# Loading the third projection weight in the attention stage, and sharing x's pair buffers with the stage that follows

## The chip, the cores and the metric

The program runs on one core of one Trainium2 chip. The metric is device time in microseconds (us) of one execution, as the median of a few runs. Five engines work side by side and meet only through semaphores: TensorE (PE, with its weight loads listed apart as PEld), VectorE (DVE), ScalarE (ACT), GpSimd (POOL) and SyncE (SP), which here issues most of the DMAs. POOL issues the DMAs that gather rows by an index.

## The reference, cut to what matters

x has 8192 rows of 512 numbers. The output is x plus two branches of xn, the layer norm of x.

```python
def step(carry, qkv):            # branch 1: 64 rows at a time, 16 heads
    M, z = carry
    q, k, v = qkv                # xn @ W_q.T, xn @ W_k.T, xn @ W_v.T
    ...
    return ((M_new, z_new), A_s)
...
weights = (x @ router_w)[..., 0] + router_b[0]   # branch 2: a router picks rows
topv, topi = jax.lax.top_k(weights, k)           # k = 1024 of 8192
...
x_sel = x[bidx, sel_idx]
hn = rmsnorm(x_sel, ln1)
q = rope(heads(hn @ wq), pos_sel)
kk = rope(heads(hn @ wk), pos_sel)
v = heads(hn @ wv)
... softmax attention among the selected rows, then
x1 = x_sel + o
x2 = x1 + jax.nn.gelu(rmsnorm(x1, ln2) @ w1) @ w2
```

The change concerns `wq`, `wk` and `wv` of branch 2, which have 512 x 512 numbers each.

## The kernel before, in words

The kernel is a row of stages, with a barrier of all engines between one and the next. `infini_attention` is the first and longest. It takes x in 32 pairs of tiles (two tiles of 128 rows), counts and chooses the rows of branch 2 on the way, and ends with `idx`, the chosen row numbers. `feed_forward` follows, and its first stage is called the projection stage here. It has eight tiles t = 0 to 7 of 128 chosen rows. For each it normalises the rows (`moments`, `scaled`), turns them round on PE (`turn_h`), splits them into a high and a low part (`high_h` on ACT, `low_h` on DVE), multiplies by the three weights (`project` on PE, 12 matmuls for each weight), and turns key and query by their angles (`turned` on DVE). The key then goes in high and low parts through `stacks` on PE. Beside that, POOL gathers rows of the causal mask, PE turns them (`masks`), ACT copies them out, and SP writes them to `mask_columns`. After it come softmax attention and the MLP.

Every weight of the projection stage exists as a high part (a rounding to float32r, made by ACT) and a low part (the raw weight less the high part, made by DVE), since PE multiplies high by high, low by high and high by low. So DVE and ACT have one pass each over 128 x 2048 numbers for each weight.

Before the change, the key and query weights are loaded by `next_weight` near the end of the attention stage, into `xin` and `xn`, x's pair buffers, which are free by then. ACT makes both high parts there (`next_high`), and DVE makes the key's low part. The stage's buffers then vanish. The projection stage therefore loads the raw query weight again and the raw value weight for the first time:

```python
for n, d in enumerate((wq_d, wv_d)):
    sp.dma_start(raw[n], d.rearrange("(c p) n -> p c n", p=P)).then_inc(s_wd[n], 16)
```

`raw[0]` lies in `xs2` (eight stage rows of 512 numbers, which later hold the turned query rows and then the MLP's raw weights), and `raw[1]` in `x1T`, whose first half is also `mcol`, the place of the mask columns. So SP's first write of mask columns waits for both low parts (`s_low`).

The order on an engine is the order in which the code is written. On DVE the projection stage opens with

```python
moments(0, 1)
scaled(0)
moments(1, 2)
low_h(0)
query_low()
angles(0)
value_low()
roots(0)
turns(0)
```

and then runs the loop over the tiles, which begins with `turned(t, KEY)`. Inside t = 0, after `low_h(1)`, stand `moments(2, 4)`, `roots(1)` and `angles(1)`. `moments(t)` waits for the gathered rows of tile t, and `angles(0)` and `angles(1)` wait for the gathered positions of tiles 0 and 1, and 2 to 7. POOL issues, one after the other: rows 0, rows 1, positions 0, positions 1, rows 2 to 7, positions 2 to 7, and then the mask rows, the first two without a wait and each later one when PE has turned the one two before it.

Of the kernel before, what the change touches and what calls it, by code (L numbers as in the profile page):

```python
# [7 lines left out]
F32 = mybir.dt.float32  # L8
# [16 lines left out]
P = 128  # L25
# [14 lines left out]
def infini_attention(nc, x, wqT, wkT, wvT, woT, beta, router_w, router_b, wq_d, wk_d, out, ident, inv, thr, idx,  # L40
                     held):
# [6 lines left out]
    T, D = x.shape  # L48
# [25 lines left out]
    with ExitStack() as ctx:  # L74
# [23 lines left out]
        xin = sb("xin", [P, 2, TILES, D])  # L98
        xn = sb("xn", [P, 2, TILES, D])
# [74 lines left out]
        next_raw = [t[:, :, :, :].rearrange("p a b n -> p (a b) n") for t in (xin, xn)]  # L174
# [16 lines left out]
        s_cw = [sem(f"s_cw{n}") for n in range(2)]  # L191
# [109 lines left out]
        def _(sp):  # L301
# [25 lines left out]
            def half(m, p, first=False, ln=True, stage1=True):  # L327
# [11 lines left out]
                if stage1:  # L339
                    shift_v(m, 1 - p)  # L340
                if AHEAD + m + 1 < NB:
                    sp.wait_ge(s_e, m + 1)
                    sp.dma_start(xe[:, :, :], x_t[AHEAD + m + 1]).then_inc(s_xe, 16)
# [13 lines left out]
            sp.wait_ge(s_od, 32 * NB)  # L357

# [927 lines left out]
def feed_forward(nc, x, maskT, positions, router_w, router_b, wq_d, wv_d, wo_d, w1_d, w2_d, ln1, ln2, ident, inv, thr, idx,  # L1286
                 held,
                 out, cols_dram):
# [20 lines left out]
    with ExitStack() as ctx:  # L1309
# [14 lines left out]
        xs2 = sb("xs2", [P, Q, D])  # L1324
# [18 lines left out]
        with ExitStack() as c1:  # L1343

            raw = (xs2[:, 0:G, :], x1T[:, 0:2, :].rearrange("p g (a n) -> p (g a) n", n=D))
# [46 lines left out]
            s_wd = [sem("s_wdq", c1), sem("s_wdv", c1)]  # L1392
# [31 lines left out]
            def _(sp):  # L1424
                sp.dma_start(l1[:, :], ln1.broadcast_to([P, D])).then_inc(s_l1, 16)
                for n, d in enumerate((wq_d, wv_d)):
                    sp.dma_start(raw[n], d.rearrange("(c p) n -> p c n", p=P)).then_inc(s_wd[n], 16)
                sp.dma_start(rw[:, :], router_w.rearrange("d a -> a d").broadcast_to([P, D])).then_inc(s_rw, 16)
                sp.dma_start(rb[:, :], router_b.broadcast_to([P, 1])).then_inc(s_rw, 16)
                for u in range(UNITS):  # L1430
                    if u == 0:
                        sp.wait_ge(s_low, 2)
# [44 lines left out]
            def _(act):  # L1477
# [48 lines left out]
                def value_high():  # L1526
                    act.wait_ge(s_wd[1], 16)
                    act.activation(vhigh[:, :, :], raw[1], ACT.Copy).then_inc(s_high, 1)

                act.activation(cos[:, 0, 0:1], ident[:, 0:1], ACT.Sin)  # L1530
                high_h(0)
                value_high()
# [26 lines left out]
            def _(dve):  # L1559
# [73 lines left out]
                def query_low():  # L1633
                    dve.wait_ge(s_wd[0], 16)
# [28 lines left out]
                dve.tensor_scalar(c2[:, 1, :], cidx[:, :], 2.0, 1.0, ALU.mult, ALU.add).then_inc(s_ci, 1)  # L1663
                moments(0, 1)
# [3 lines left out]
                query_low()  # L1668
                angles(0)
                value_low()  # L1670
# [761 lines left out]
def build(nc, x, wqT, wkT, wvT, woT, beta, maskT, positions, router_w, router_b, wq, wk, wv, wo, w1, w2, ln1, ln2,  # L2432
# [4 lines left out]
    with ExitStack() as ctx:  # L2437
# [6 lines left out]
        infini_attention(nc, x, wqT, wkT, wvT, woT, beta, router_w, router_b, wq, wk, out, ident, inv, thr, idx,  # L2444
# [45 lines left out]
```

## Time and profile before

| what | value |
|---|---|
| median of 3 runs | 1964.27 us (1963.94 to 1964.94) |
| the profiled execution, its own time | 1966.73 us |
| its span from first to last instruction | 1965.0 us |
| mean granted TensorE clock | 0.981 of full speed |
| PE busy | 1861.8 us (95%) |
| DVE busy | 1443.1 us (73%) |
| ACT busy | 875.6 us (45%) |
| POOL busy | 151.0 us (8%) |

Times in the rows below are us from the first instruction. The attention stage ends at about 1288, and the projection stage runs from there to about 1418. A timeline row gives the start, the length, the engine, the line, the operation, what it writes and reads, how many instructions were merged, and in brackets how long the engine sat idle before it and what released it. An "issue" in brackets is idle time in which the engine waited for nothing that the profile shows.

### The profile page before, as it was taken

How to read it: one execution, taken by the hardware profiler on the slowest of the kernel's cores; microseconds unless marked ns; L12 is line 12 of the kernel's file. 1: busy time of each engine (PE TensorE's matmuls, PEld its weight loads, DVE VectorE, ACT ScalarE, POOL GpSimd, SP SyncE). 2: the span in 40 equal slices, each digit the busy share in tenths (PEclk: the TensorE clock that was granted, in tenths of full speed). 3: DMA queues.
4: the chain of work that ended last, by engine and by line, in shares of the span. 5: the costliest groups of instructions: out<-in, count | busy, mean ns of one | idle time of the engine just before them, and what ended most of it. 6: DMA issues, size and time to landing. Idle time of an engine off the chain costs nothing. (4 is left out here: it accounts for less than half of the span.)

```text
span 1965.0 us, 72355 instructions
## 1 busy us (share of the span) xinstructions
PE 1861.8 (95%) x32380; PEld 1579.7 (80%) x32380; DVE 1443.1 (73%) x3478; ACT 875.6 (45%) x1494; POOL 151.0 (8%) x179
## 2 busy tenths in 40 slices
PE   6999999999999999999999999859899999888998
PEld 6888888888888888888888888647777777667997
DVE  6888788888887777787777777557588788876222
ACT  4343444334443434444344344225588788754110
POOL 1000000000000000000000000141100000001000
PEclk9999999999999999999999999779999999999999
DMA  4112111211121121112111211036500000015000
GB/s 146 46 46 70 59 52 46 78 57 46 57 73 41 36 57 41 41 35 57 46 36 35 62 41 62 30 129 192 157 32 13 12 12 23 12 44 161 11 12 22
DMA packets 65668, 109.52 MB, mean 56 GB/s; under 512 B 4736, under 2 KB 25232, under 8 KB 65360
## 3 DMA queue, kind: packets, MB, share of 16 engines
q1 hardware_dynamic: 59584, 85.74, 14.0%
q0 software_dynamic: 5776, 19.15, 3.1%
q8 instruction: 257, 4.21, 0.9%
q14 instruction: 51, 0.42, 0.1%
HBM read 60.31 MB, written 27.26 MB: 45 GB/s over the span
## 5 line engine op out<-in xcount | busy, mean ns | idle before, releaser
L1021 PE MATMUL proj<-xnT_high,held 128*128 128x256 f32 x1536 | 235.2, 289 | 2.8 <-DVE xnT_low L749 2.1
L1021 PEld LDWEIGHTS proj<-xnT_high,held 128*128 128x128 f32 x1536 | 203.7, 191 | 8.8 <-DVE xnT_low L749 2.6
L425 POOL TENSOR_TENSOR As<-T 128x512 f32<-128x512 f32 x64 | 84.1, 1315 | 1178.9 <-DVE T L844 1178.9
L1021 PE MATMUL proj<-xnT_low,held 128*128 128x256 f32 x1024 | 163.7, 281 | 0.0
L2017 DVE CUSTOM_DVE_ANT_0 Sm<-Sp,held 128x1023 f32<-128x1023 f32 x128 | 155.5, 1215 | 8.4 <-DVE xs L2005 2.0
L1915 ACT ACTIVATE Sm<-Sm,least 128x1023 f32<-128x1023 f32 x128 | 146.7, 1146 | 14.2 <-DVE least L2017 13.4
L1021 PEld LDWEIGHTS proj<-xnT_low,held 128*128 128x128 f32 x1024 | 140.2, 190 | 0.0
L2070 PE MATMUL Sp<-KS,held 128*128 128x512 f32 x256 | 94.4, 451 | 29.8 <-DVE least L2017 25.6
L484 ACT ACTIVATE Pq<-Pq 128x1024 f32<-128x1024 f32 x64 | 67.9, 1061 | 121.2 <-DVE Pq L813 120.9
L464 ACT ACTIVATE QT<-proj 128x512 f32<-128x512 f32 x64 | 38.1, 595 | 181.7 <-PE proj L1021 181.7
L1967 DVE COPY PTs<-Tp 128x512 f32<-128x512 f32 x128 | 88.3, 690 | 29.6 <-PE Tp L2082 29.1
L443 ACT ACTIVATE DV<-proj 128x512 f32<-128x512 f32 x64 | 38.2, 597 | 159.9 <-PE proj L1031 159.9
L2291 PEld LDWEIGHTS Sp<-held,KS 128*128 128x128 f32 x768 | 96.7, 193 | 9.2 <-issue 3.6
L2291 PE MATMUL Sp<-held,KS 128*128 128x256 f32 x768 | 98.4, 285 | 5.4 <-DVE held L2276 2.7
L1888 ACT ACTIVATE PTs<-Tp 128x512 f32<-128x512 f32 x128 | 76.1, 595 | 52.7 <-PE Tp L2078 49.5
L2351 PE MATMUL yb<-w2m,held 128*128 128x512 f32 x384 | 94.5, 396 | 0.0
L464 ACT ACTIVATE KT<-proj 128x512 f32<-128x512 f32 x64 | 38.3, 598 | 104.6 <-PE proj L1021 104.6
L2351 PEld LDWEIGHTS yb<-w2m,held 128*128 128x128 f32 x384 | 70.3, 189 | 14.8
L2078 PE MATMUL Tp<-ident,Sm 128*128 128x128 f32 x512 | 81.0, 281 | 1.0 <-ACT PTs L1888 0.9
L1021 PE MATMUL proj<-xnT_high,wk_low 128*128 128x256 f32 x512 | 81.3, 280 | 0.4 <-issue 0.4
L813 DVE TENSOR_TENSOR Pq<-S,mx 128x1024 f32<-128x1024 f32 x64 | 78.4, 1225 | 2.2
L1184 PE MATMUL proj<-wo_high,AT_high 128*128 128x512 f32 x256 | 77.8, 426 | 1.7 <-DVE AT_low L756 1.6
(322 smaller groups left out, 4360.1 us busy)
## 6 DMA issues: line engine op xcount, KB each, us to landing
VS<-DV SPq DMA_DIRECT2D x64, 264.0 KB, 3.9
xin<-in_x SPq DMA_DIRECT2D x32, 512.0 KB, 4.8
out_rows<-xu SPq DMA_DIRECT2D x64, 256.0 KB, 2.0
mask_columns<-x1T SPq DMA_DIRECT2D x16, 512.0 KB
xs<-in_w SPq DMA_DIRECT2D x16, 512.0 KB, 4.0
xe<-in_x SPq DMA_DIRECT2D x15, 512.0 KB, 3.5
QT<-in_wqT SPq DMA_DIRECT2D x1, 1024.0 KB, 6.1
KT<-in_wkT SPq DMA_DIRECT2D x1, 1024.0 KB, 9.3
```

Source lines behind the costliest of these rows:

```text
L425: pool.tensor_tensor(As[:, :], T1[:, :], T2[:, :], ALU.add).then_inc(s_as, 1)
L464: act.activation(raw[:, pn, 2 * k:2 * k + 2, :], v, ACT.Copy, scale=scale)
L813: dve.tensor_tensor(Pq[:, :, :, :].rearrange("p g j k -> p j g k"), s_half(a), mx[:, :, :].rearrange("p j (g o) -> p j g o", o=1).broadcas ...
L1021: ins = pe.matmul(bank[:, g * BT:g * BT + BT], w[hw][:, c, o:o + P], xnT[hx][:, c, :], start=n + c == 0, stop=n == 2 and c == G - 1)
L1184: ins = pe.matmul(bank[:, :], AT[ha][:, g, :], wo[hw][:, g, :], start=n + g == 0, stop=n == 2 and g == G - 1)
L1915: act.activation(Sm[:, h % 4, 0:KC], Sm[:, h % 4, 0:KC], ACT.Exp, bias=least[:, h % 4:h % 4 + 1], scale=-1.0, accum_out=rsum[:, b, h:h + 1 ...
L1967: dve.tensor_copy(PTs[:, slot(t, h), 4:8, :], Tp[1][:, :].rearrange("p (k q) -> p k q", k=4))\
L2017: dve.tensor_tensor_reduce(Sm[:, h % 4, 0:KC], Sp[h % 2][:, 0:KC], mc[:, b, 0:KC], 1.0, 3.0e38, ALU.add, ALU.min, least[:, h % 4:h % 4 + 1])\
L2070: ins = pe.matmul(Sp[h % 2][:, u * 512:u * 512 + 512], QS[:, h, :], KS[:, h, u * 512:u * 512 + 512], start=True, stop=True)
L2078: ins = pe.transpose(Tp[0][:, k * P:k * P + P], Sm[:, h % 4, k * P:k * P + P], ident[:, :])
L2291: ins = pe.matmul(self.hb[n % 4][:, e * self.NT:e * self.NT + self.NT], self.w1[hw][:, c, f * P:f * P + P], self.xT[hx][:, c, :], start=m ...
L2351: ins = pe.matmul(yb[(u % 2) * QU + q][:, :], gT[hg][:, n % 4, e, q * P:q * P + P], w2[hw][:, f, :], start=f + m == 0, stop=f == FC - 1 an ...
```

## The change

`xs2` is now made ahead of both functions and handed to both. In the attention stage its first four rows are `xin` and its last four are `xn`. The raw query weight, loaded into `xn`, therefore survives the end of the attention stage. A third load brings the raw value weight into the place of `xin`, once ACT has made the key's high part and DVE its low part. The projection stage issues no weight loads, ACT makes the value's high part before `high_h(0)`, and DVE makes both low parts before everything else that is long. SP's first write of mask columns no longer waits for the low parts.

```diff
-        xin = sb("xin", [P, 2, TILES, D])
-        xn = sb("xn", [P, 2, TILES, D])
+        xin, xn = [xs2[:, 2 * TILES * i:2 * TILES * i + 2 * TILES, :].rearrange("p (b a) d -> p b a d", a=TILES)
+                   for i in range(2)]
...
-        next_raw = [t[:, :, :, :].rearrange("p a b n -> p (a b) n") for t in (xin, xn)]
+        next_raw = [xs2[:, 0:G, :], xs2[:, G:2 * G, :], xs2[:, 0:G, :]]
...
+                if m == NB - 1:
+                    sp.wait_ge(s_ch, 1)
+                    sp.wait_ge(s_cl, 1)
+                    next_weight(VALUE, wv_d)
                 if AHEAD + m + 1 < NB:
...
             sp.wait_ge(s_od, 32 * NB)
+            sp.wait_ge(s_cw[VALUE], 16)
...
-            raw = (xs2[:, 0:G, :], x1T[:, 0:2, :].rearrange("p g (a n) -> p (g a) n", n=D))
+            raw = (xs2[:, G:2 * G, :], xs2[:, 0:G, :])
...
-                for n, d in enumerate((wq_d, wv_d)):
-                    sp.dma_start(raw[n], d.rearrange("(c p) n -> p c n", p=P)).then_inc(s_wd[n], 16)
...
-                    if u == 0:
-                        sp.wait_ge(s_low, 2)
...
                 def value_high():
-                    act.wait_ge(s_wd[1], 16)
                     act.activation(vhigh[:, :, :], raw[1], ACT.Copy).then_inc(s_high, 1)
...
+                value_high()
                 high_h(0)
-                value_high()
                 waves(0)
...
                 def query_low():
-                    dve.wait_ge(s_wd[0], 16)
...
+                query_low()
+                value_low()
                 moments(0, 1)
                 scaled(0)
                 moments(1, 2)
                 low_h(0)
-                query_low()
                 angles(0)
-                value_low()
                 roots(0)
                 turns(0)
```

On DVE, at the head of the projection stage, the order before was this. `wq_low` and `wv_low` are the two low parts, `cidx` and `c` the clipped indices, `hn` the normalised rows of a tile, `hnT` their turned form, `fb` the banks of PSUM, and `pos` the positions.

```order
L1661 TENSOR_SCALAR cidx<-idx 128x8
L1662 TENSOR_SCALAR c<-cidx 128x8 [waits s_st]
L1663 TENSOR_SCALAR c<-cidx 128x8 [waits s_st]
L1610 BN_STATS stats<-xs 128x6 [waits s_xg0]
L1613 BN_AGGR mv<-stats 128x2 [waits s_st]
L1630 SCALAR_TENSOR_TENSOR hn<-xs,mv,ln 128x512 [waits s_l1,s_st]
L1610 BN_STATS stats<-xs 128x6 [waits s_xg1]
L1613 BN_AGGR mv<-stats 128x2 [waits s_st]
L1643 TENSOR_TENSOR hnT<-fb,hnT 128x512 [waits s_hh,s_st]
L1635 TENSOR_TENSOR wq_low<-xs,held 128x2048 [waits s_wdq]
L1578 CAST posf<-pos 128x2 [waits s_pos0]
```

After the change the same place reads as follows.

```order
L1659 TENSOR_SCALAR c<-cidx 128x8 [waits s_st]
L1631 TENSOR_TENSOR wq_low<-xs,held 128x2048
L1635 TENSOR_TENSOR wv_low<-xs,wv_high 128x2048 [waits s_high]
L1606 BN_STATS stats<-xs 128x6 [waits s_xg0]
L1609 BN_AGGR mv<-stats 128x2 [waits s_st]
L1626 SCALAR_TENSOR_TENSOR hn<-xs,mv,ln 128x512 [waits s_l1,s_st]
L1606 BN_STATS stats<-xs 128x6 [waits s_xg1]
L1609 BN_AGGR mv<-stats 128x2 [waits s_st]
L1639 TENSOR_TENSOR hnT<-fb,hnT 128x512 [waits s_hh,s_st]
L1574 CAST posf<-pos 128x2 [waits s_pos0]
```

Both low parts moved ahead of the first wait for gathered rows (`s_xg0`), and the query's waits for no load any more.

On SP, around the barrier between the two stages, the order before was this. The rows of `out_rows` are the last stores of the attention stage.

```order
L319 DMA out_rows<-xu 128x512 [waits s_free0]
L319 DMA out_rows<-xu 128x512 [waits s_od,s_free0] x3
L74 UNCONDITIONAL_BRANCH [waits s_od]
L1423 UNCONDITIONAL_BRANCH [waits barrier_Pool_Activation_PE_DVE_SP_release]
L1425 DMA ln<-in_ln 128x512
L1427 DMA xs<-in_wq 128x4x512
L1427 DMA x1T<-in_wv 128x4x512
L1428 DMA rw<-in_router_w 128x512
L1429 DMA rb<-in_router_b 128x1
L1436 DMA mask_columns<-x1T 128x8x128 [waits s_mc,s_low]
```

After the change SP reads here as follows.

```order
L319 DMA out_rows<-xu 128x512 [waits s_od,s_free0]
L325 DMA xs<-in_wv 128x4x512 [waits s_od,s_cl,s_ch]
L319 DMA out_rows<-xu 128x512 [waits s_free0]
L319 DMA out_rows<-xu 128x512 [waits s_od,s_free0]
L74 UNCONDITIONAL_BRANCH [waits s_od,s_cw2]
L1425 UNCONDITIONAL_BRANCH [waits barrier_Pool_Activation_PE_DVE_SP_release]
L1427 DMA ln<-in_ln 128x512
L1428 DMA rw<-in_router_w 128x512
L1429 DMA rb<-in_router_b 128x1
L1434 DMA mask_columns<-x1T 128x8x128 [waits s_mc] x16
```

The value weight's load moved between the second and the third of the last four stores, and the query weight's second load is gone. The orders of PE and POOL are the same before and after.

## Rows read from the trace of the kernel before

**Rows 1.** Stretches: us; PE, PEld, DVE, ACT, POOL busy (instructions); clock, DMA share, GB/s
```profile
1290.00:1300.00 10.00, 1.12 (x4) 0.72 (x4) 2.42 (x5) 0.21 (x2) 7.56 (x9) 0.50 0.90 318
...
1311.00:1325.00 14.00, 10.17 (x46) 8.18 (x46) 12.53 (x42) 4.62 (x7) 3.14 (x4) 0.76 0.23 76
1325.00:1340.00 15.00, 14.18 (x81) 11.71 (x80) 13.81 (x42) 7.79 (x15) 2.78 (x3) 1.00 0.49 150
...
1360.00:1380.00 20.00, 19.81 (x122) 16.90 (x121) 10.95 (x22) 11.84 (x22) 4.93 (x5) 1.00 0.79 223
```

**Rows 2.** Timeline of DVE in the projection stage's first part
```profile
1289.02 0.17 DVE L1663 TENSOR_SCALAR c<-cidx 128x8 uint32<-128x8 uint32 x1
...
1296.95 0.70 DVE L1610 BATCH_NORM_STATS2 stats<-xs 128x6 f32<-128x512 f32 x1 [7.75 <-DMA xs<-in_x,idx]
...
1300.56 0.69 DVE L1643 TENSOR_TENSOR hnT<-fb,hnT 128x512 fp32r<-128x512 f32 x1 [1.09 <-issue]
1301.17 2.28 DVE L1635 TENSOR_TENSOR wq_low<-xs,held 128x2048 fp32r<-128x2048 f32 x1
1303.37 0.16 DVE L1578 CAST posf<-pos 128x2 f32<-128x2 int32 x1
...
1306.11 2.29 DVE L1639 TENSOR_TENSOR wv_low<-x1T,wv_high 128x2048 fp32r<-128x2048 f32 x1
1308.31 0.16 DVE L1619 TENSOR_SCALAR vv<-mv 128x2 f32<-128x2 f32 x1
...
1311.44 0.69 DVE L1654 TENSOR_TENSOR qa<-fb,coss 128x512 f32<-128x512 f32 x1
...
1322.34 0.17 DVE L1578 CAST posf<-pos 128x6 f32<-128x6 int32 x1
...
1333.01 0.68 DVE L1643 TENSOR_TENSOR hnT<-fb,hnT 128x512 fp32r<-128x512 f32 x1
```

**Rows 3.** Timeline of ACT there
```profile
1289.86 0.20 ACT L1530 ACTIVATE cos<-ident 128x1 f32<-128x1 f32 x1
...
1301.98 1.91 ACT L1528 ACTIVATE wv_high<-x1T 128x2048 fp32r<-128x2048 f32 x1 [1.53 <-issue]
```

**Rows 4.** Timeline of POOL there: the DMAs that it issues
```profile
1289.33 1.02 POOL L1441 DMA_INDIRECT xs<-in_x,idx  x1 [14.24 <-POOLq L74]
...
1302.29 1.98 POOL L1445 DMA_INDIRECT pos<-in_positions,cidx  x1 [0.30 <-issue]
...
1307.11 2.11 POOL L1445 DMA_INDIRECT pos<-in_positions,cidx  x1 [0.30 <-issue]
...
1312.03 0.94 POOL L1462 DMA_INDIRECT x1T<-in_maskT,c  x1 [0.30 <-issue]
```

**Rows 5.** DMA issues: what, by whom, how many, median us from issue to landing
```profile
xs<-in_x,idx POOLq DMA_INDIRECT x8, 6.2
...
held<-mask_columns,cidx POOLq DMA_INDIRECT x8, 4.4
xs<-out_rows,idx POOLq DMA_INDIRECT x8, 3.6
```

**Rows 6.** Timeline of PE there
```profile
1298.71 1.12 PE L1730 MATMUL fb<-ident,hn 128*128 128x128 f32 x4 [13.36 <-DVE hn L1630]
1301.31 6.39 PE L1747 MATMUL fb<-held,hnT 128*128 128x512 f32 x20 [1.48 <-DVE hnT L1643]
...
1314.24 0.66 PE L1730 MATMUL fb<-ident,hn 128*128 128x128 f32 x4 [2.80 <-DVE hn L1630]
1315.93 3.83 PE L1769 MATMUL fb<-ident,kst 128*128 128x128 f32 x16 [1.02 <-DVE kst L1683]
...
1323.29 1.03 PE L1722 MATMUL ft<-ident,x1T 128*128 128x128 f32 x8
```

**Rows 7.** Timeline of the attention stage's tail: one row of DVE, one of SP
```profile
1257.78 2.28 DVE L743 TENSOR_TENSOR held<-xin,held 128x2048 fp32r<-128x2048 f32 x1
...
1278.54 7.90 SPq L319 DMA_DIRECT2D out_rows<-xu  x2
```

More of the change, by code:

```diff
@@ L37, in bm, with infini_attention @@
     return t.rearrange("p (o n) -> p o n", o=1).broadcast_to([t.shape[0], m, t.shape[1]])
-def infini_attention(nc, x, wqT, wkT, wvT, woT, beta, router_w, router_b, wq_d, wk_d, out, ident, inv, thr, idx,
-                     held):
+def infini_attention(nc, x, wqT, wkT, wvT, woT, beta, router_w, router_b, wq_d, wk_d, wv_d, out, ident, inv, thr, idx,
+                     held, xs2):
     T, D = x.shape
@@ L190, in infini_attention @@
         s_wl = sem("s_wl")
-        s_cw = [sem(f"s_cw{n}") for n in range(2)]
+        s_cw = [sem(f"s_cw{n}") for n in range(3)]
         s_ch = sem("s_ch")
@@ L1283, in rotation_steps, with feed_forward @@
     return np.float32(1.0) / np.float32(10000.0) ** (np.arange(0, DK, 2, dtype=np.float32) / np.float32(DK))
-def feed_forward(nc, x, maskT, positions, router_w, router_b, wq_d, wv_d, wo_d, w1_d, w2_d, ln1, ln2, ident, inv, thr, idx,
-                 held,
-                 out, cols_dram):
+def feed_forward(nc, x, maskT, positions, router_w, router_b, wo_d, w1_d, w2_d, ln1, ln2, ident, inv, thr, idx,
+                 held, xs2, out, cols_dram):
     D = x.shape[1]
@@ L1323, in feed_forward @@
         l2 = l1
-        xs2 = sb("xs2", [P, Q, D])
         x1T = sb("x1T", [P, G, K])
@@ L1391, in feed_forward @@
             s_rw = sem("s_rw", c1)
-            s_wd = [sem("s_wdq", c1), sem("s_wdv", c1)]
             s_high = sem("s_high", c1)
@@ L2443, in build @@
                 for n in range(3)]
-        infini_attention(nc, x, wqT, wkT, wvT, woT, beta, router_w, router_b, wq, wk, out, ident, inv, thr, idx,
-                         held)
-        feed_forward(nc, x, maskT, positions, router_w, router_b, wq, wv, wo, w1, w2, ln1, ln2, ident, inv, thr, idx,
-                     held,
+        xs2 = ctx.enter_context(nc.sbuf_tensor("xs2", [P, K // P, x.shape[1]], F32))
+        infini_attention(nc, x, wqT, wkT, wvT, woT, beta, router_w, router_b, wq, wk, wv, out, ident, inv, thr, idx,
+                         held, xs2)
+        feed_forward(nc, x, maskT, positions, router_w, router_b, wo, w1, w2, ln1, ln2, ident, inv, thr, idx,
+                     held, xs2,
                      out, cols_dram)
```

## The prediction, made before the changed kernel was run

> **What bounds the kernel now.** I read first the stretches of the projection stage, then the timeline of each engine at its head. In the attention stage TensorE is busy throughout and the change takes nothing off it, so what can move lies after 1288 us. From 1290 to 1300 nothing works: PE is busy 1.12 of 10 us at half clock (0.50, 1.2 GHz), DVE 2.42, while the DMA engines are at a share of 0.90 [rows 1]. DVE sits idle 7.75 us for the first gathered rows, which land at 1296.95, and PE 13.36 us for what DVE makes of them [rows 2, 6]. Then DVE sets the pace: 12.53 of 14 us from 1311 to 1325 and 13.81 of 15 to 1340, with PE waiting for it 2.80 and 1.02 us at 1314 to 1316 [rows 1, 6]. Later PE does (19.81 of 20 us from 1360, DVE 10.95) [rows 1]. A DVE that is earlier at its first `turned` by some us should therefore hand PE an earlier start, and since all later work, masks included, follows PE, that is kept to the end. The number to find is how much earlier `turned(0, KEY)` begins, now 1311.44 [rows 2].
>
> **The change part by part.**
>
> *Attention stage, no cost.* SP waits for DVE's low part of the key, which ends at 1257.78 + 2.28 = 1260.06, and loads the value weight. Behind that wait on SP stands only the store that is issued at 1278.54, 18 us later [rows 7]. The new wait ahead of the barrier is for a load begun at 1260. The slowest landing that I have in sight is a gather's 6.2 us [rows 5]; even twice that is long past by 1288. If the 18 us of cover were gone, the store and the barrier would be late by what is missing. No instruction is added: two 1 MB loads leave the projection stage, one enters the attention stage.
>
> *DVE's two low parts move into the idle time.* They stand at 1301.17 and 1306.11, and the next starts come at 1303.37 and 1308.31, so each costs the path 2.20 us, together 4.4 us [rows 2]. In the new place, the query's low part starts when DVE ends its three index operations, 1289.02 + 0.17 = 1289.2, and ends at 1291.4. The value's needs ACT's high part: ACT is free at 1290.06 and takes 1.91 us, to 1292.0 [rows 3], so the low part runs from 1292.0 to 1294.2. DVE is then free 2.7 us before the rows landed so far.
>
> *The gathers lose their company and gain an obstacle.* POOL's first issue takes 1.02 us from 1289.33, and its rows land 6.6 us after the issue's end, at 1296.95, amid the 2 MB of weights [rows 2, 4]. The same kind of gather elsewhere, with little beside it, lands 3.6 us after its start, so some 2.65 us after its end, an issue being 0.94 us [rows 4, 5]. Against that, the two issues of position DMAs that began while DVE was inside a low part took 1.98 and 2.11 us in place of 0.94, and both ended 0.82 us after that DVE operation [rows 2, 4]. A low part now runs from 1289.2, just ahead of the first issue. I therefore let that issue end at 1291.4 + 0.8 = 1292.3 and its rows land at 1294.9. The second issue begins 0.3 us later, inside the value's low part (1292.0 to 1294.2), ends at 1295.1, and its rows land at 1297.7. Positions 0 and 1 are issued to 1296.3 and 1297.6; by the same 2.65 us (an estimate, since no row shows a position's landing) they land at 1300.2.
>
> The Trainium skill, "SBUF — State Buffer", section "SBUF: two separate sides", states the same in its rule that a DVE instruction with two SBUF inputs and a GpSimd instruction that reads SBUF lock each other out; the stretched issues agree. Its practical consequences add, marked as inferred, that a `tensor_tensor` takes only the read interface while descriptor generation needs the write interface, so that it should not stall such a DMA. By that, the first rows would not be held up; it is rival 2, and the 1.98 and 2.11 us speak against it.
>
> *The sum.* `low_h(0)` came 1300.56 - 1296.95 = 3.6 us after the first rows [rows 2], so 1298.5; `moments(1, 2)` ahead of it, about 1 us, cannot begin before 1297.7, which makes it 1298.7, ended 1299.4. `angles(0)` waits for the positions until 1300.2. It takes 1306.11 - 1303.37 = 2.74 us, and from there to `turned` it is 1311.44 - 1308.31 = 3.13 us [rows 2], so `turned(0, KEY)` begins at 1306.1 in place of 1311.4: **5.3 us earlier**. Of this, 4.4 us are the two passes and 0.9 us the earlier gathers.
>
> *Does PE follow?* It starts the first projection at 1299.4 in place of 1301.31. The whole of it ran to 1311.44 (2.80 us of idle before 1314.24) [rows 6], half clock included, so now to some 1310.0 (half clock may last longer, since it began earlier). Then `turn_h(1)` follows without its 2.80 us of waiting, and `stacks(0)` begins near 1310.7 in place of 1315.93, 5.2 us earlier. PE keeps up. The 16 transposes and the next 12 matmuls then bring it to `masks(1)` at about 1317, from 1323.29. Here a new wait comes up. POOL is 3.5 us late after its second issue, gets back the 1.04 and 1.17 us of the two stretched issues, and may lose some to DVE's shorter passes in the loop, which its issues of positions now meet; I allow 1.3 us for that, an estimate of about one stretched issue. So the first mask gather starts at about 1314.3 in place of 1312.03, and by 4.4 us it lands at 1318.5 [rows 4, 5]. PE idles 1.5 us. DVE next needs PE at `low_h(2)`, 1333.01 before and 1327.7 now [rows 2]; my PE arrives some 0.4 us ahead. The last positions land at 1316.5, and `angles(1)` needs them at 1322.34 - 5.3 = 1317.0 [rows 2]. Both covers are thin, 0.4 and 0.5 us.
>
> The sum against the profiled execution's own time is 1966.73 - 5.3 = 1961.4 us. That execution was 2.5 us above the median of the runs, so against the median it is 1964.27 - 5.3 = **1959.0 us**. A measurement of this kernel can tell about 0.2% from no change, which is 3.9 us.
>
> **The rivals.**
>
> 1. *The gathers land no earlier, only the passes are saved.* If what delays the first rows is not the weights, or both passes hold up the first issue one after the other (its end 1295.0, rows 1297.7, everything 0.8 us later), the gain is 4.4 or 3.6 us: 1959.9 to 1960.7. For it: the gap between the passes is only 0.6 us. Against it: the DMA share of 0.90 falls away with the weights [rows 1].
> 2. *The passes don't stall the issues.* The first rows land at 1290.35 + 2.65 = 1293.0, DVE takes them at 1294.2, positions are there by 1296.8, and `angles(0)` begins at 1298.6. DVE would gain 7 us, but `low_h(1)` then waits for PE, which loses time at half clock; about 6.3 us are left: 1958.0. The stretched issues speak against it [rows 4].
> 3. *PE is held at the masks and its clock falls.* After the 2.80 and 1.02 us of idle at 1311 to 1316 the granted clock of 1311 to 1325 was 0.76 on average, that is 3.4 us of 14 lost [rows 1, 6]. The forecast takes these waits away, but puts 1.5 us in their place a little later. If that brings the clock down for half as long, PE loses 1.7 us, against 0.4 us of cover; with a mask gather 0.5 to 1 us later too, the gain falls to 2.2 to 3.6 us: 1960.7 to 1962.1.
> 4. *It is hidden.* If PE were the pace from 1316 on, a DVE that is earlier would change less: PE is busy 14.18 of 15 us from 1325 [rows 1]. But PE itself is freed by the same amount, so a gain under 1 us (1963.3 and above) needs another pace, which I do not see.
> 5. *Slower: POOL's queue becomes the pace.* `angles(1)` needs the last positions, twelve issues behind positions 1. Each us that they are late beyond 1317.0 is a us on DVE. Were every one of the twelve stretched like the worst in sight (2.11 - 0.94 = 1.17 us), of which I have counted 1.3 us in all, they would be 12.7 us later, less 0.5 us of cover: 5.3 - 12.2, a loss of 6.9 us, 1971.2. It decides from 5.8 us of further delay. Against it: two of the fourteen issues after the first two were stretched that far, and the long passes are past by 1294.2.
>
> **How the numbers follow.** The forecast, gains of 4.5 to 6 us, has 0.48; rival 1 0.16; rival 2 0.08; rival 3 0.17; rival 4 0.06; rival 5 0.05 (of which a loss over 3.9 us is nearly all). Faster by over 0.2%: 0.48 + 0.08 + 0.11 of rival 1 = 0.67. The same: 0.05 of rival 1, rival 3 and rival 4 = 0.28. Slower: 0.05. The range from 1957.4 to 1962.6 reaches past rival 2 by 0.6 us and past rival 3 by 0.5 us, for other half-clock stretches that an earlier start may shift, and leaves out rivals 4 and 5 and the tails.
>
> **What would show it.** After: no weight load after the barrier; DVE in its low parts at 1289.2 and 1292.0 (counted from the same barrier); POOL's first two issues of some 3.0 and 2.5 us; first rows landed near 1295; `turned` 5.3 us earlier; a granted clock above 0.9 from 1311 to 1325; a short wait of PE for the first mask rows; and from 1360 on the same rows as before, 5.3 us earlier. The prediction is wrong if the first rows land at 1297 or later, if `angles(1)` or `low_h(2)` waits for more than 1 us, or if the attention stage itself ends at another time.

## The result, and the profile after

| | before | changed |
|---|---|---|
| median, 22 runs each on one chip | 1964.32 us (1960.91 to 1966.99) | 1968.51 us (1964.81 to 1974.94) |
| ratio, 95% interval | | 1.0020 (1.0014 to 1.0027) |
| profiled execution, span | 1965.0 us | 1965.6 us |
| mean granted TensorE clock | 0.981 | 0.979 |

The changed kernel takes 4.2 us more. The forecast was 5.3 us less, so the prediction was wrong in size and in sign here.

The barrier after the attention stage is read at DVE's first index operation. It stands at 1285.56 us here and stood at 1288.61 before. In the twenty traces of this study it lies between 1281.9 and 1288.6 (two traces of the kernel before: 1288.61 and 1285.00), so that difference is scatter. From here on, "+n" is a time in us after this barrier.

The timeline of DVE at the head of the stage, in the changed kernel, to be held against [rows 2]:

```profile
1285.56 0.17 DVE L1657 TENSOR_SCALAR cidx<-idx 128x8 uint32<-128x8 uint32 x1 [2.60 <-PEq L74]
...
1286.05 2.28 DVE L1631 TENSOR_TENSOR wq_low<-xs,held 128x2048 fp32r<-128x2048 f32 x1
1288.85 2.29 DVE L1635 TENSOR_TENSOR wv_low<-xs,wv_high 128x2048 fp32r<-128x2048 f32 x1 [0.52 <-ACT wv_high L1525]
1291.62 0.69 DVE L1607 BATCH_NORM_STATS2 stats<-xs 128x6 f32<-128x512 f32 x1 [0.48 <-DMA xs<-in_x,idx]
...
1297.06 0.17 DVE L1575 CAST posf<-pos 128x2 f32<-128x2 int32 x1 [0.98 <-DMA pos<-in_positions,cidx]
...
1305.02 0.69 DVE L1650 TENSOR_TENSOR qa<-fb,coss 128x512 f32<-128x512 f32 x1 [2.24 <-remote]
...
1312.86 0.69 DVE L1650 TENSOR_TENSOR qa<-fb,coss 128x512 f32<-128x512 f32 x1 [2.65 <-remote]
```

The head is as forecast: both low parts at once, first rows at +6.07 (before +8.34), positions at +11.5. Then `turned(0, KEY)` (1305.02) waits 2.24 us and `turned(0, QUERY)` (1312.86) 2.65 us. The releaser is given as "remote": a semaphore that the instruction waits for was updated just before it began, but no instruction that makes this update had ended within 1.5 us ahead of that. The timeline of POOL in the changed kernel, for [rows 4]:

```profile
1286.28 2.95 POOL L1439 DMA_INDIRECT xs<-in_x,idx  x1 [14.52 <-POOLq L74]
1289.53 2.46 POOL L1439 DMA_INDIRECT xs<-in_x,idx  x1 [0.30 <-issue]
...
1311.47 0.94 POOL L1460 DMA_INDIRECT x1T<-in_maskT,c  x1 [0.30 <-issue]
```

The timeline of PE there, for [rows 6]:

```profile
1303.32 1.10 PE L1743 MATMUL fb<-wq_low,hnT 128*128 128x512 f32 x4
1304.26 2.04 PE L1743 MATMUL fb<-wv_high,hnT 128*128 128x512 f32 x8
1306.13 1.10 PE L1743 MATMUL fb<-wv_low,hnT 128*128 128x512 f32 x4
1307.92 0.66 PE L1726 MATMUL fb<-ident,hn 128*128 128x128 f32 x4 [0.70 <-DVE hn L1627]
1310.27 1.09 PE L1765 MATMUL fb<-ident,kst 128*128 128x128 f32 x8 [1.68 <-issue]
1316.97 1.94 PE L1765 MATMUL fb<-ident,kst 128*128 128x128 f32 x8 [5.61 <-ACT KS L1520]
```

The timeline of ACT, where it has waited for `turn_h(1)`:

```profile
1315.17 0.60 ACT L1493 ACTIVATE hnT<-fb 128x512 fp32r<-128x512 f32 x1 [6.23 <-remote]
```

PE ends the query's last four matmuls at 1304.42, and DVE gets the bank at 1312.86. PE ends the transposes of `turn_h(1)` at 1308.58, and ACT starts on them at 1315.17, 6.6 us later, with nothing else to wait for. PE then stands still for 5.61 us, because ACT has not emptied a bank. Half clock begins 26 us after the barrier, as before the change, but lasts 10.2 us in place of 6.8 (0.63 granted from 1311 to 1325). I call this **late signals**: the work is done by its record, and those who wait for it learn of it microseconds later. POOL's last issue of its stream ends at 1312.41. The kernel before has no such row of PE here.

The trace also keeps the time of each semaphore update, and there the lateness can be read directly. The update for the query's matmuls, which end at +18.9, is recorded at +27.28, and DVE starts at +27.30. The next four updates of PE, for work that ends at +21.67 (the value), +23.02 (`turn_h(1)`), +25.36 and +25.80 (the key's transposes), are recorded at +29.52, +29.58, +29.64 and +29.70, and ACT starts at +29.61. So the four were held back and came 0.06 us apart.

### The profile page after: what moved, and what is told of

It is laid out like the page before. It is cut to its first block and busy times, and to the rows that moved or that the text cites. A ratio compares the mean times of both kernels' runs of the same rounds, so it can differ in the third digit from the quotient of the medians.

```text
span 1965.6 us, 72355 instructions
## 1 busy us (share of the span) xinstructions
PE 1864.1 (95%) x32380; PEld 1583.4 (81%) x32380; DVE 1442.9 (73%) x3478; ACT 875.7 (45%) x1494; POOL 153.6 (8%) x179
## 5 line engine op out<-in xcount | busy, mean ns | idle before, releaser
L2074 PE MATMUL Tp<-ident,Sm 128*128 128x128 f32 x512 | 82.3, 284 | 0.9 <-ACT PTs L1884 0.8
L2078 PE MATMUL Tp<-ident,Sm 128*128 128x128 f32 x512 | 79.0, 278 | 1.6 <-DVE PTs L1963 1.6
```

Source lines behind the costliest of these rows:

```text
L2074: ins = pe.transpose(Tp[0][:, k * P:k * P + P], Sm[:, h % 4, k * P:k * P + P], ident[:, :])
L2078: ins = pe.transpose(Tp[1][:, (k - 4) * P:(k - 4) * P + P], Sm[:, h % 4, k * P:k * P + P], ident[:, :])
```

## The experiments

The expectations speak of calls: a call is one session on one chip, in which some kernels and the kernel before were timed side by side, and ratios are to that. The table has what the traces showed. "Signals" counts the semaphore updates of PE, DVE and ACT that have a record at the end of their instruction (within 0.15 us), out of those that their instructions make, between +12 and +28. Of the others, some are recorded late and some not at all. The columns with the names of two operations have the time at which they begin. "Stage" runs from the barrier to the first instruction of softmax attention on DVE, and "rest" from there to the end.

| call | kernel | ratio (95%) | signals | `turned(0, KEY)` | `high_h(1)` | stage | rest |
|---|---|---|---|---|---|---|---|
| given | before | 1 | 41/50 | +22.8 | +26.3 | 132.5 | 543.9 |
| result | changed | 1.0020 (1.0014 to 1.0027) | 14/44 | +19.5 | +29.6 | 133.9 | 546.1 |
| 1 | e0 changed | 1.0022 (1.0011 to 1.0032) | 17/46 | +17.2 | +29.4 | 133.9 | 546.0 |
| 1 | e1 | 0.9999 (0.9987 to 1.0011) | 45/59 | +20.7 | +24.2 | 130.3 | 546.3 |
| 1 | e2 | 1.0021 (1.0011 to 1.0031) | 18/49 | +19.5 | +29.1 | 134.0 | 546.5 |
| 1 | e3 | 1.0001 (0.9991 to 1.0011) | 38/50 | +22.8 | +26.4 | 132.5 | 543.6 |
| 2 | e4 | 0.9989 (0.9979 to 0.9999) | 61/61 | +18.5 | +22.0 | 128.1 | 540.7 |
| 2 | e7 | 0.9977 (0.9965 to 0.9990) | 67/67 | +18.5 | +22.1 | 128.6 | 540.1 |
| 2 | e5 | 1.0015 (1.0004 to 1.0026) | 71/71 | +17.5 | +22.1 | 133.5 | 541.7 |
| 2 | e6 | 0.9969 (0.9956 to 0.9983) | 71/71 | +17.2 | +22.1 | 127.1 | 541.7 |
| 3 | e8 changed | 1.0012 (1.0003 to 1.0021) | 12/47 | +18.0 | +29.4 | 133.4 | 545.2 |
| 3 | e9 | 1.0020 (1.0011 to 1.0030) | 13/47 | +18.1 | +29.5 | 134.0 | 546.1 |
| 3 | e10 (as e6) | 0.9993 (0.9984 to 1.0002) | 18/48 | +17.3 | +26.7 | 130.9 | 545.5 |
| 3 | e11 (as e7) | 0.9992 (0.9981 to 1.0003) | 27/57 | +18.6 | +25.2 | 131.3 | 545.4 |
| 4 | e12 changed | 0.9983 (0.9970 to 0.9996) | 71/71 | +17.2 | +22.1 | 127.1 | 541.5 |
| 4 | e13 (as e5) | 1.0019 (1.0007 to 1.0031) | 73/73 | +17.0 | +22.1 | 133.5 | 541.6 |
| 4 | e14 | 0.9978 (0.9967 to 0.9990) | 73/73 | +17.0 | +22.1 | 126.9 | 541.5 |
| 4 | e15 | 0.9971 (0.9960 to 0.9983) | 71/71 | +17.2 | +22.1 | 127.1 | 541.5 |
| 5 | e16 (as e14) | 0.9987 (0.9975 to 0.9998) | 30/59 | +18.8 | +23.0 | 129.2 | 545.8 |
| 6 | e17 before | 0.9999 (0.9987 to 1.0011) | 50/50 | +22.7 | +26.2 | 132.2 | 540.2 |

### Call 1: which part of the change is it

*e0, the changed kernel again.*

> The changed kernel once more, unaltered. In its first profile the head of the projection stage gained what was forecast (first turned key 6.4 us earlier, 3.4 us from the barrier), and then DVE waited 2.2 and 2.7 us and ACT 6.2 us for the first tile's projections, whose matmul records end up to 8 us before PE's semaphores tell of them. If that stall belongs to the change (theory 1), it is there again, at the same place, and the ratio to before is 1.001 to 1.004. If it was chance in one profile (theory 2), it is gone from this one, and the loss in the timed runs has another place: then the projection stage is 4 to 6 us shorter than before and another stage longer.

Measured: 1967.57 us beside 1964.24, with the late signals again. It is no accident of one trace.

*e1, the order on DVE and ACT undone.*

```diff
                 act.activation(cos[:, 0, 0:1], ident[:, 0:1], ACT.Sin)
-                value_high()
                 high_h(0)
+                value_high()
...
-                query_low()
-                value_low()
                 moments(0, 1)
                 scaled(0)
                 moments(1, 2)
                 low_h(0)
+                query_low()
                 angles(0)
+                value_low()
```

> The changed kernel with the old order on DVE and ACT: the low parts back behind low_h(0) and angles(0), the value's high part behind high_h(0). Loads and buffers stay as changed. If the new order makes the stall (theory 1, order), it is gone: some 1 to 2 us under before, because the first rows land earlier by 2 to 3 us with no weights beside them. If the absence of the loads, or the attention stage's part, makes it (theory 3), the time stays 3 to 5 us above before.

*e2, the new order, but with two loads of 1 MB in the stage again (of no use). ACT waits for them ahead of its first copy of mask columns, which the lines below leave out.*

```diff
+                sp.dma_start(V[:, 4:8, :], wo_d.rearrange("(c p) n -> p c n", p=P)).then_inc(s_dum, 16)
+                sp.dma_start(x1T[:, 0:2, :].rearrange("p g (a n) -> p (g a) n", n=D),
+                             wo_d.rearrange("(c p) n -> p c n", p=P)).then_inc(s_dum, 16)
```

> The changed kernel with two loads of 1 MB back at the head of the projection stage, into places that nothing reads (V rows 4 to 7 and mcol, waited for by ACT ahead of its first copy of mask columns); the order of the low parts stays new. If the order makes the stall, the time stays at or above the changed kernel's (first rows 2 us later: +1 to +3 us). If the stall needs PE to start early, ahead of the time at which it started before, the later rows take it away and the time falls by 2 to 5 us.

*e3, both: the old order and the two loads.*

> Both undone: the old order and two loads of 1 MB back at the head of the projection stage. What is left of the change is the attention stage's part (x's pair buffers in the shared tile, the third load there) and the place of the buffers. If the projection stage holds the whole effect, this is within 1 us of before. If the attention stage's part costs (theory 3), it is 3 to 5 us above before.

Measured: 1964.39, 1967.43 and 1964.58 us. Where the buffers lie and the load in the attention stage cost nothing that the timing can tell (e3). Taking the loads out brings the old order's head 2.2 us forward (e1 against e3 in the table), but not the time, where I had expected 1 to 2 us. The new order costs 2.9 to 3.2 us with and without loads, though in e2 PE begins 2.9 us later than in e0. So it is the order, and it comes with late signals. In the old order PE's signals are on time in this stage, in the same call and beside the same stream of POOL. In e1 PE ends its three projections at +15.95, +18.89 and +21.70, as in e0 (+16.00, +18.81, +21.61), and their updates are recorded at +15.96, +18.91 and +21.72, while e0 has the last two at +23.55 and +29.26. PE's transposes end at +24.11, and ACT begins at once, in the midst of POOL's stream (the timelines of PE, ACT and POOL in e1):

```profile
1305.34 0.66 PE L1726 MATMUL fb<-ident,hn 128*128 128x128 f32 x4 [1.75 <-DVE hn L1627]
1306.04 0.60 ACT L1493 ACTIVATE hnT<-fb 128x512 fp32r<-128x512 f32 x1 [0.33 <-issue]
1306.99 0.94 POOL L1460 DMA_INDIRECT x1T<-in_maskT,c  x1 [0.30 <-issue]
```

The given trace of before and e3 show the same: PE's updates here are recorded as its work ends, all but one in each trace, which has no record.

### Call 2: half of the order, and pauses of POOL

On DVE, *e4* moves only the query's low part and *e7* only the value's; the other stands where it stood before. (In e7 PE also waits for both low parts before the first that it reads, since the query's is now the second.) *e5* and *e6* are the changed kernel with one wait more on POOL:

```diff
+                pool.wait_ge(s_ht, 2)           # e5
                 for q in range(FIRST, Q):
                     places(q)
+                pool.wait_ge(s_ht, 2)           # e6
                 for u in range(UNITS):
```

> Kernel: the changed kernel, but DVE makes only the query's low part at the head of the projection stage; the value's stands between angles(0) and roots(0) again, as before. What is known by now: the changed kernel and its repeat show PE's signals (query done, turn_h(1) done) arriving up to 8 us after the last matmul of them in the trace, and only until 29 us after the barrier; with the old order on DVE and ACT this is absent. Theory A (the signals are late because POOL's issues and their packets are in the way while DVE and PE are both at work; one long DVE pass in the middle takes DVE out for 2.3 us and stretches a POOL issue): half the gain and half the stall or less, turned(0, KEY) some 18.5 us after the barrier of the stage, high_h(1) between 25 and 29, time 1964 to 1967. Theory B (it is the value's low part or ACT's value_high at the head that brings it about): high_h(1) at about 24 us, no late signals, 1961 to 1963. Theory C (PE stands still by itself once it runs through without a wait): the stall as in the changed kernel, high_h(1) at 29, 1967 to 1968.

> Kernel: the changed kernel, but DVE makes only the value's low part at the head of the projection stage; the query's stands between low_h(0) and angles(0) again, as before (PE waits for both low parts before the first that it reads). Theory A: as with the query alone, half or less of the stall, 1964 to 1967. Theory B, if the value's low part at the head is the cause: the stall as in the changed kernel, high_h(1) at 29 us after the barrier, 1967 to 1968. Theory C: the stall as well, 1967 to 1968.

> Kernel: the changed kernel, but POOL waits before the gathers of positions 2 to 7 until PE has turned tile 1 (turn_h(1)), so that between some 16.5 and 22 us after the barrier POOL issues nothing. Theory A (POOL's issues and packets are in the way): PE's signals arrive within 0.3 us of their matmuls, turned(0, QUERY) and high_h(1) come 20 and 22.5 us after the barrier in place of 24 and 29; angles(1) then waits 1 to 2 us for the last positions; 1961 to 1963. Theory B or C (DVE's or PE's own doing): the signal of turn_h(1) is as late as before, so POOL goes on only at 29, the last positions land at 39 and angles(1) waits some 5 us: 1972 to 1976.

> Kernel: the changed kernel, but POOL waits before its first two gathers of mask rows (2 x 512 KB, issued at 24.7 and 25.9 us after the barrier) until PE has turned tile 1. Theory A in the form that the big mask gathers hold the signals up: turn_h(1)'s signal arrives by 25 us, high_h(1) at 25 in place of 29.5, and 1964 to 1965. Theory A in the form that the issues of positions or all of POOL's issues do it: the signal comes when POOL has stopped at 24.5 us, so 25 too, but turned(0, QUERY) is late as before. Theory B or C: the signal at 29 as before; masks gathered 3 us later than now, PE waits for them 3 us, 1968 to 1971.

Measured: 1958.89, 1956.09, 1963.55 and 1956.62 us beside 1960.58. No signal is late in any of the four. `high_h(1)` comes at +22.0 to +22.1, even in e6, whose added wait is over before POOL gets to it. Up to that point e6 does what the changed kernel does, so the change alone does not bring the late signals about. None of the times expected for the four came (e5's is 0.55 us beyond the nearest). All the expectations reckon with late signals in the changed kernel, so what they were to separate could not be judged here. e5 shows the price of a pause at the wrong place: `angles(1)` waits for the last positions, and the stage takes 6.4 us more than in e6.

### Calls 3 and 4: the kernel or the call

> Kernel: the changed kernel once more, unchanged, beside the three below. The first four experiments ran on one chip, the second four on another, and on the second none of the four shows a late signal of PE, though in e6 the added wait was already over when POOL came to it, so that up to 25 us after the barrier that kernel did just what the changed one does. Theory D (the late signals belong to the chip or the moment, and with them only the new order is hurt): on a chip without them the changed kernel shows high_h(1) at 22 us, and a ratio of 0.997 to 0.998 as e6; on a chip with them high_h(1) at 29 us and 1.002. Theory E (they belong to the changed kernel as it stands, its mask gathers or where its instructions lie in memory): high_h(1) at 29 us and 1.002 on any chip, with the three below free of them.

*e9* is e6 with `s_ht` at 1, a wait that is long over.

> Kernel: e6 with its added wait made empty: before the first mask gathers POOL waits until PE has turned tile 0, which is long past. It differs from the changed kernel by one instruction in POOL's stream and by nothing in time. Theory D: as the changed kernel in the same call, within 0.05%. Theory E, if the place of instructions decides: no late signals, ratio 0.997, and the changed kernel 1.002.

> Kernel: e6_masks_paced again (the first two gathers of mask rows wait until PE has turned tile 1). Theory D: as the changed kernel in the same call where there are no late signals; where there are, it is the test of whether the mask gathers share in them: high_h(1) at 25 to 26 us and a ratio near 1.000 if they do, 29 us and 1.003 if not. Theory E: 0.997 and no late signals.

> Kernel: e7_value_only again (only the value's low part at the head, the query's between low_h(0) and angles(0)). Theory D: on a chip without late signals 0.9975 to 0.999, a little slower than the changed kernel, since one pass of 2.2 us is on the path; on a chip with them it may be the faster of the two, as the old order was. Theory E: 0.9977 on any chip.

Measured in call 3: 1967.50, 1968.90, 1965.16 and 1964.52 us beside 1965.88. All four have late signals, e9 as much as the changed kernel, so theory E is out. In e11, half of the new order, `high_h(1)` begins 3.0 us after PE's transposes, in place of 7.3 us in e8. e10, whose mask gathers wait, gets the signal of `turn_h(1)` 2.7 us earlier than e8 does. The timeline of POOL in e10:

```profile
1309.67 0.95 POOL L1443 DMA_INDIRECT pos<-in_positions,cidx  x1 [0.31 <-issue]
1313.01 1.04 POOL L1461 DMA_INDIRECT x1T<-in_maskT,c  x1 [2.39 <-remote]
```

The timeline of ACT in e10:

```profile
1312.78 0.60 ACT L1494 ACTIVATE hnT<-fb 128x512 fp32r<-128x512 f32 x1 [5.50 <-remote]
```

POOL's stream ends at 1310.62, which is +24.6 (+26.6 in e8), and the signal reaches ACT and POOL 2.2 to 2.4 us after that. This pointed at POOL's stream. In e14 POOL pauses earlier, and what is needed last is gathered last:

```diff
-                for q in range(FIRST, Q):
+                for q in range(FIRST, 4):
                     rows(q)
                 for q in range(FIRST, Q):
                     places(q)
+                pool.wait_ge(s_ht, 2)           # not in e15
                 for u in range(UNITS):
                     t, hh = u // 2, u % 2
+                    if u == 2:
+                        for q in range(4, Q):
+                            rows(q)
```

> Kernel: the changed kernel again, unchanged, as the mark for this call: on two of three chips so far PE's signals came late (high_h(1) 29.4 us after the barrier, ratio 1.001 to 1.002), and on the third the neighbours of this kernel were free of it (22.07 us, 0.997). Theory D expects one of the two here, by the chip: 1.001 to 1.002 with 29.4, or 0.997 with 22.07. Theory E expects 29.4 and 1.002 on any chip.

> Kernel: e5_new_paced again (POOL waits before positions 2 to 7 until PE has turned tile 1), so far run only on a chip without late signals. Theory A (POOL's stream of issues and gathers is in the way of PE's signals, on the chips that show it): POOL stops at 17 us after the barrier, the signals come some 2 us later, by 19 to 20, and high_h(1) starts at 22 to 23 us even where the changed kernel has it at 29.4. Theory C (PE's or DVE's own doing): the signals are as late as in the changed kernel, high_h(1) at 27 to 29, and all that follows POOL 5 us later still, ratio 1.005 and above. On a chip without late signals both say 1.0015 as measured, since angles(1) then waits for the last positions.

> Kernel: the changed kernel with POOL's order changed: rows 0, 1, positions 0, 1, rows 2, 3, positions 2 to 7, then a wait until PE has turned tile 1, the first two gathers of mask rows, rows 4 to 7, and the other mask rows. POOL stops at 19 us after the barrier. Theory A: high_h(1) at 22 to 23 us on any chip, no wait for positions, mask rows landed at 27: 0.996 to 0.998 everywhere. Theory C: high_h(1) at 27 to 29 on a chip with late signals, masks some 5 us late, 1.003.

> Kernel: e14 without its wait: POOL issues all of it in one stream, up to 27 us after the barrier as in the changed kernel, with the mask rows already at 19. Theory A: on a chip with late signals high_h(1) at 27 to 29.4 us and 1.001 to 1.002, like the changed kernel; without them 22.07 and 0.997. Theory C: the same. It shows what the pause itself is worth beside the new order of POOL's issues.

Measured: 1957.87, 1964.38, 1958.72 and 1955.71 us beside 1962.49. This call had no late signals, so it could not test the stream, and the changed kernel, unchanged, is now faster than before: 0.9983. The calls bear chip numbers, and calls 1 and 4 bear the same one, as do calls 3 and 6; each pair has one call of each kind. So a call's kind does not follow the number. The timeline of ACT in e12, where nothing is "remote":

```profile
1309.51 0.60 ACT L1493 ACTIVATE hnT<-fb 128x512 fp32r<-128x512 f32 x1 [1.67 <-PE fb L1726]
```

That of DVE in e12:

```profile
1304.67 0.69 DVE L1650 TENSOR_TENSOR qa<-fb,coss 128x512 f32<-128x512 f32 x1
...
1309.02 0.68 DVE L1650 TENSOR_TENSOR qa<-fb,coss 128x512 f32<-128x512 f32 x1
```

That of PE in e12:

```profile
1308.88 0.60 PE L1726 MATMUL fb<-ident,hn 128*128 128x128 f32 x4
...
1317.21 1.09 PE L1718 MATMUL ft<-ident,x1T 128*128 128x128 f32 x8 [2.04 <-DMA x1T<-in_maskT,c]
```

PE's transposes end at 1309.48 and ACT starts at 1309.51, while POOL is issuing all the time. Here `turned(0, KEY)` stands at +17.22, and PE waits 2.04 us for the first mask rows.

### Call 5: POOL's stream stops early, in a call with late signals

> Kernel: e14_rows_last again (rows 4 to 7 gathered last, and a pause of POOL from 19 us after the barrier until PE has turned tile 1). The fourth call showed the changed kernel free of late signals (e12), though it ran under the same chip number as the first call, which showed them: they belong to the call, not to a chip's number. So far the calls of the result, of e0 to e3 and of e8 to e11 had them, those of e4 to e7 and of e12 to e15 had not. If this call has them (update records missing from 12 us after the barrier on): theory A (POOL's stream of issues and gathers is in the way) puts high_h(1) at 22 to 24 us and the ratio at 0.996 to 0.998, theory C at 27 to 29 us and 1.000 to 1.003. If the call has none (no record missing), both say 22.07 us and 0.998, and the question between A and C stays open.

Measured: 1962.29 us beside 1965.97, and half of the updates (29 of 59) have no record in their place, so this call has late signals. The timeline of POOL in e16:

```profile
1300.28 0.94 POOL L1443 DMA_INDIRECT pos<-in_positions,cidx  x1 [0.30 <-issue]
1305.51 1.53 POOL L1464 DMA_INDIRECT x1T<-in_maskT,c  x1 [4.29 <-PE fb L1730]
```

That of DVE in e16:

```profile
1303.17 0.69 DVE L1658 TENSOR_TENSOR krow<-qa,qb 128x512 f32<-128x512 f32 x1 [0.78 <-DVE qb L1657]
```

That of PE in e16:

```profile
1304.58 0.66 PE L1730 MATMUL fb<-ident,hn 128*128 128x128 f32 x4 [0.70 <-DVE hn L1631]
```

That of ACT in e16:

```profile
1305.27 0.60 ACT L1497 ACTIVATE hnT<-fb 128x512 fp32r<-128x512 f32 x1 [0.32 <-PE fb L1730]
...
1804.99 1.06 ACT L2272 ACTIVATE held<-x1T 128x1024 fp32r<-128x1024 f32 x1 [8.86 <-remote]
```

POOL stops at 1301.22, which is +19.0. From +12 to there only 6 of 32 updates have a record. From +20 until POOL goes on, every one has. The last late ones are in 2 us after POOL's stop: two of DVE's own at +20.87 and +20.89, and PE's for the query at +20.94, 2.1 us after the matmuls. Then PE's transposes end at 1305.24, and ACT starts at 1305.27. `high_h(1)` is at +23.0, as theory A says, and not at +27 to +29. The ratio, 0.9987, lies above the 0.996 to 0.998 that went with theory A, and below theory C's 1.000 to 1.003. The pause stops POOL's issues and its packets together, so which of the two is in the way was not separated. The last row is a control in the same trace, in the MLP: there POOL issues eight gathers in one stream again, and ACT again waits for a "remote" signal.

### Call 6: the kernel before with a trace of its own

> Kernel: the kernel before, unchanged, with a trace of its own. Its trace of before comes from a call in which update records are missing (21 to 23 us after the barrier), so it may hold a small loss of the same kind. Theory D with A: in a call without missing records the old order has lost something too, at most the 2 us or so by which its medians in such calls lie lower (1960.6 and 1962.5 us against 1964.2 to 1966.0): no half-clock stretch at 26 us after the barrier, and the softmax stage begins 130 to 132 us after it in place of 132.5. In a call with missing records all is as in the trace of before (high_h(1) at 26.3, softmax stage at 132.5). The ratio is 1.000 in both.

Measured: 1960.14 us beside 1960.50, no record missing. My expectation that the stage might gain up to 2 us was wrong: it takes 132.2 us, as in the first trace (132.5). The half-clock stretch at +26 is there too (6.8 us), where I had expected none. Nearly all that the kernel before loses to late signals is in the rest, 543.9 against 540.2 us, and that in one place: the gap between the two traces goes from 0.1 to 4.0 us between +515 and +535. The timeline of PE there, in the given trace of before:

```profile
1807.85 2.96 PE L2291 MATMUL Sp<-held,KS 128*128 128x256 f32 x24
1810.65 2.96 PE L2351 MATMUL yb<-w2m,held 128*128 128x512 f32 x12
1816.35 4.63 PE L2291 MATMUL Sp<-held,KS 128*128 128x256 f32 x24 [2.74 <-DVE held L2276]
```

That of ACT in the given trace:

```profile
1813.98 1.06 ACT L2272 ACTIVATE held<-x1T 128x1024 fp32r<-128x1024 f32 x1 [8.14 <-remote]
```

That of POOL in the given trace:

```profile
1812.76 0.95 POOL L2418 DMA_INDIRECT xs<-out_rows,idx  x1 [0.30 <-issue]
```

The same stretch in e17, PE:

```profile
1804.78 2.96 PE L2291 MATMUL Sp<-held,KS 128*128 128x256 f32 x24
1807.58 2.96 PE L2351 MATMUL yb<-w2m,held 128*128 128x512 f32 x12
1810.38 2.97 PE L2291 MATMUL Sp<-held,KS 128*128 128x256 f32 x24
```

And ACT in e17:

```profile
1807.78 1.06 ACT L2272 ACTIVATE held<-x1T 128x1024 fp32r<-128x1024 f32 x1 [5.00 <-PE Sp L2291]
```

In e17 PE's 24 matmuls end at 1807.74 and ACT starts at 1807.78. In the given trace they end at 1810.81, ACT starts at 1813.98, 3.2 us late, and POOL's last of eight issues ends at 1813.71. Every trace of the calls with late signals has this wait, 3.0 to 3.9 us, and in every trace of the others ACT starts 0.04 us after PE ends. PE loses 2.74 us of waiting and some more at half clock (its next 24 matmuls take 4.63 in place of 2.97 us).

## Why the prediction was wrong

**The step that failed** is "Does PE follow?", with its "PE keeps up". The forecast let DVE and ACT go on in the moment in which PE's matmuls end. In the calls with late signals they could not: in the changed kernel's trace `turned(0, QUERY)` came 8.4 us and `high_h(1)` 6.6 us after PE's work, just when PE's updates were recorded. No rival had this. Rival 5 named POOL's queue as the pace of a loss, but by late positions, and those were in time.

**The earlier steps held.**
- *Low parts in the idle time:* at +0.49 and +3.29, forecast +0.6 and +3.4.
- *Gathers held up by them:* issues of 2.95 and 2.46 us, forecast 3.0 and 2.5, ending 0.90 and 0.85 us after DVE's operation. First rows +6.07, forecast +6.3; positions +11.5, forecast +11.6. Rival 2 is out. The Trainium skill, "SBUF — State Buffer", section "SBUF: two separate sides", infers that a `tensor_tensor` does not stall such a DMA, and these rows speak against it again.
- *The sum for `turned(0, KEY)`:* e12 against e17, both free of late signals, gives +17.22 against +22.70, so 5.5 us; forecast 5.3.
- *A new wait at the masks:* 2.04 us in e12, forecast 1.5. The prediction's own terms add up to more than it says: 1312.03 + 3.5 - 1.04 - 1.17 + 1.3 = 1314.6 for the first mask gather in place of 1314.3, landed at 1319.0 in place of 1318.5, a wait of 2.0 us. That the measured wait is the same is luck in part: counted from its barrier, e12's gather begins 0.7 us before 1314.6, and PE is there as much earlier.

**Kept to the end: mostly.** Without late signals the stage takes 127.1 in place of 132.2 us, 5.1 us less. The rest takes 1.3 us more (541.5 against 540.2), and by traces, which are of two calls, 3.8 us remain. The timing gives 0.17% (0.04 to 0.30), 3.3 us (0.8 to 5.9). The 1.3 us go with more half clock: e12 has 10.2 us of it where the stage ends, e17 has 6.8, and e12 has a further 3.4 us near +463. What brings it there was not tried. So in a call of this kind the forecast of faster is right, and its 5.3 us lie inside the interval, though above the 3.3 measured.

**The loss with late signals.** The stage takes 133.9 in place of 132.5 us and the rest 546.1 in place of 543.9: 3.6 us by traces, 4.2 us by time. Against the calls without late signals the new order loses 6.8 us in the stage (133.9 against 127.1), the old one 0.3 (132.5 against 132.2). It isn't that the same lateness meets more slack in the old order: there PE's signals are not late in this stage at all (e1, e3, before). The 2.2 us in the rest go with 11 us more of half clock; the wait in the MLP is the same in both. What the runs show is that in such a call the new order suffers (e0, e2, e8, e9), that half of it suffers less (e11), that the old order does not, and that stopping POOL's stream brings the signals back (e16; in part e10).

**What stays open.** That POOL's stream is needed for the late signals rests on one trace with a pause in it (e16), on e10 in part, and on the place in the MLP, which is again beside a stream; but in some calls it does no harm at all. What differs between the calls I do not know. Nor do I know what it is in the new order. One difference can be read: the old order has a low part of 2.3 us on DVE within the stream (in e1 at +15.3) that stretches an issue of POOL to 2.2 us, and the new order has none after +5.6; no run tried it alone. The signals also do not always wait for the end of the stream: in e11 `high_h(1)` started 2.5 us before it, and `turned(0, QUERY)` got its signal within it in e0, e8 and e9. That PE's own matmuls ran later than their records, instead of the signals being late, does not fit the traces: four updates of PE, for work whose ends lie at least 1.3 us apart, are recorded within 0.18 us, in the changed kernel and in e0, e2, e8, e9 and e10 alike. One rival is untested: late signals and missing records always come together, and each run on record, timed ones too, has a span and a clock of the recording with it. Whether an execution without any recording has late signals, no run here can tell.

The best version is e14 (e16): 0.9978 without late signals and 0.9987 with them, where the changed kernel has 0.9983 and 1.0012 to 1.0022. Of the versions tried in both kinds of call it alone has its interval below 1 in both. That it beats e6 (0.9969 without, 0.9993 with, as e10) is not shown, since the intervals overlap.

## What to carry to other kernels

Look for places where an engine will wait for another's signal while GpSimd issues a long row of gathers. There an edit that is right by the sum of its waits can lose more than it saves, because it can decide whether the signals come on time. Issue first what is needed first, and let the rest wait for a signal of the engine that must be heard. Repeat a measurement of 0.2% in another call before believing its sign: one and the same kernel gave 1.0022 and 0.9983 here.

## What the runs showed of the hardware that was not expected

- While GpSimd issues gathers one after the other (0.95 us each, 0.30 us apart), other engines' semaphore updates can arrive late, up to 8.4 us after PE's work here and 3.0 to 3.9 us in the MLP. With it, updates have no record in their place (12 to 18 of 44 to 49 have one in the new order), and most of these lie in such streams: up to the barrier, where there are none, at most one of 3910 is missing in any trace.
- Updates that were held back come in a burst: in six traces four of PE come 0.06 us apart, the first of them 1.5 to 2.7 us after the stream ended.
- It is a matter of the call: four calls had it (given and result taken as one), three had not.
- It is also a matter of what the other engines do: in the same call, beside the same stream, PE's updates were on time with DVE's old order (e1, e3).
- From 2 us after GpSimd had fallen silent, updates were on time again (e16).
